# First x rows as four loads, per-channel constants turned by PE, epsilon added by POOL

## The chip, the cores and the metric

The kernel runs on one core of one Trainium2 chip. The time is device microseconds of one execution; the median of three runs of the kernel before is 579.78 us (579.25 to 581.91).

## The reference

Four batches of 512 rows of 512 numbers (x) go through one layer: a gated state-space mixer, whose hidden input is a second tensor (ctx) and whose gate is the normalised x, and then a feed-forward network with weights cut to -1, 0, 1. Both are added to x.

```
h   = in_proj_w @ ctx                                  # 256 -> 512 channels
u   = silu(conv4(h, conv_w) + conv_b)                  # 4 taps per channel, causal
dt, Bm, Cm = split(x_proj_w @ u)                       # 16 + 16 + 16 rows
delta = softplus(dt_proj_w @ dt + dt_proj_b)
state = state * exp(delta * -exp(A_log)) + (delta * u) * Bm      # scan over 512 rows, 16 states
y   = sum_n(state_n * Cm_n) + D * u
x   = x + y * silu(layernorm(x))                       # eps 1e-5
n   = layernorm(x)
g   = silu(quant(n) @ ternary(w_gate)) * (quant(n) @ ternary(w_up))
x   = x + quant(rms_norm(g, ln_w)) @ ternary(w_down)
```

quant rounds each row to 8 bits by its largest absolute value; ternary divides a weight by its mean absolute value, rounds and cuts to [-1, 1].

## The kernel before, in words

Channels lie on the partitions, 4 blocks (KE) of 128; a batch has 512 rows, in 4 blocks (KL) of 128. All engines' programs are written out by hand, one function per engine, and each engine runs its instructions in the order in which they are written; semaphores alone tie them together. SP issues most loads, in one queue.

The opening, some 90 us, prepares everything that the scan wants:

- SP loads the weights of the input projection (in_s), ctx of batch 0, the taps (cw, 512 x 4), the bias (cb, one number per channel), x of batch 0 (load_x(0), one load of 1 MB), and then in turn weights w_all of the feed-forward part (1 MB each), ctx and x of batches 1 to 3 (lines 289 to 310).
- POOL makes the identity and small constants, and then issues eight loads of its own (L416): the projection xp_t in two pieces into xp_s, the delta weights and their bias twice into dt_s, the decay a_log, and D (dsk, one number per channel). xp_s and dt_s were filled with zeros by DVE before (L816, L817; semaphore started). For each batch b it raises the variance plus epsilon to -0.5 (x_power, L432) and normalises x in place (x_norm, L439, 4 instructions). Then it makes skip, the identity scaled by D (L462), and du, the product of delta and u (L449).
- PE projects (conv(b, h), L1096: two channel blocks each, 4 matmuls of 128x512, which run as 8 passes), two calls for each batch, with three pairs of PSUM banks in turn; a pair is free again when DVE has read it. Then come the projection of u (project, L1106), turns and the projection of delta. keep_warm(n) (L1151) are matmuls of ones whose result nobody reads.
- ACT writes the last tap times the projection plus the bias (last_tap, L565), and DVE adds the other three taps (conv, L834: 6 instructions for one call, 12 for a batch). ACT also sums and scales weights (L581, L588), and applies silu (L572). ACT's first wait is for taps and bias (conv_loaded), ahead of everything.
- DVE takes the statistics of x of batch b (x_stats(b): bn_stats L866 four times, bn_aggr L869 four times, epsilon added at L871), and the order on DVE is x_stats(0), both calls of conv of batch 0, x_stats(1), conv of batch 1, x_stats(2), the mean of the first weight, conv(2, 0), x_stats(3), the rest of conv. Behind that it sums and cuts weights (L841, L858, L861), whose stores SP issues, and copies the turned du (L877).

Then the scan runs over 4 batches times 16 states, and the feed-forward part over 16 blocks of rows. Neither is touched by the change, except that the sources of D and of the decay are ready at another time.

## Time and profile before

| what | us |
|---|---|
| median of three runs (lowest, highest) | 579.78 (579.25, 581.91) |
| the profiled execution, its own time | 580.82 |
| its span | 578.9 |
| PE, DVE, ACT, POOL busy | 540.0, 535.8, 512.3, 468.7 |
| mean granted TensorE clock | 0.997 |

The profile is of one execution. The span runs from the first instruction to the last; the execution's own time has the start and the end around it, 1.9 us more. A wait is shown with the engine and line that ended it. The chain of waits follows the work that ended last back to the start. PE's float32 matmuls run as several passes, and each is shown as an instruction; PEld is PE's weight load. The issue of a load (SPq) is short, and its landing is told separately, in us from the issue.

### The profile page before, as it was taken

The page shows a single profiled execution, that of the slowest core. Times are in us where ns is not written, and L with a number is a line of the kernel's source. Part 1 is how long each engine was busy: PE and PEld are TensorE (multiplying, and loading weights), DVE is VectorE, ACT ScalarE, POOL GpSimd, SP SyncE. Part 2 cuts the span into 40 slices and gives each one's busy share as a digit, 9 for nine tenths or more (in the row PEclk, how much of TensorE's full clock was granted, in tenths as well). Part 3 has the DMA queues.
Part 4 walks back from the last instruction along what each step waited for, and adds up shares of the span by engine and source line. Part 5 has one row for each costly group of instructions (what it writes and reads, how often), then busy time and mean ns, then how long its engine had stood idle before and what let it go on. Part 6 is the DMA issues. An engine that isn't in the chain of part 4 may idle for free.

```text
span 578.9 us, 10285 instructions
## 1 busy us (share of the span) xinstructions
PE 540.0 (93%) x3684; PEld 402.5 (70%) x3684; DVE 535.8 (93%) x774; ACT 512.3 (89%) x755; POOL 468.7 (81%) x198
## 2 busy tenths in 40 slices
PE   5898988899999999999999889999989999999996
PEld 2335476899998999989999789987434444444443
DVE  3999989999999999999999999999899989899873
ACT  1899999999999999989999799999877878878784
POOL 4889374999999899999999999995666665765772
PEclk9999999999999999999999999999999999999999
DMA  8992690111222823127432276252442442533521
GB/s 274 410 382 74 217 315 23 55 57 58 66 61 58 196 84 102 55 56 165 128 92 57 63 173 209 74 152 86 78 102 68 96 96 65 109 83 76 116 54 55
DMA packets 62194, 68.64 MB, mean 119 GB/s; under 512 B 41137, under 2 KB 41137, under 8 KB 59969
## 3 DMA queue, kind: packets, MB, share of 16 engines
q1 hardware_dynamic: 59776, 63.59, 36.8%
q0 software_dynamic: 2368, 4.40, 4.6%
q8 instruction: 30, 0.49, 0.3%
q14 instruction: 20, 0.16, 0.1%
HBM read 50.02 MB, written 8.52 MB: 101 GB/s over the span
## 4 chain that ended last, share of the span: by engine, by line
PE 36%; DVE 22%; ACT 20%; POOL 8%; issue 8%; DMA 5%; SPq 0%; DVEq 0%; ACTq 0%; POOLq 0%
PE ps L1268 9%; ACT arena L704 8%; PE ps L1233 8%; POOL arena L473 7%; PE ps L1217 6%; PE ps L1278 6%; ACT arena L629 6%; DVE arena L834 5%; DVE arena L923 5%; PE ps L1220 4%; DMA arena<-c_rows 2%; DVE bst_x L866 2%; DMA arena<-x 1%; ACT arena L626 1%; ACT arena L779 1%
## 5 line engine op out<-in xcount | busy, mean ns | idle before, releaser
L473 POOL TENSOR_TENSOR arena<-arena 128x2048 f32<-128x2048 f32 x62 | 282.2, 4616 | 12.9 <-DVE arena L923 10.1
L923 DVE TENSOR_TENSOR_SCAN arena<-arena,ps 128x512 f32<-128x512 f32 x256 | 286.9, 1197 | 1.8 <-ACT arena L704 0.2
L704 ACT ACTIVATE arena<-arena,a_neg 128x512 f32<-128x512 f32 x256 | 164.9, 709 | 8.2 <-DVE arena L923 8.1
L1233 PE MATMUL ps<-ident,arena 128*128 128x128 f32 x1024 | 155.1, 275 | 6.2 <-DVE arena L933 3.3
L1233 PEld LDWEIGHTS ps<-ident,arena 128*128 128x128 f32 x1024 | 119.9, 141 | 10.4 <-POOL arena L473 5.1
L1268 PE MATMUL ps<-arena 128*128 128x512 bf16 x512 | 113.5, 379 | 1.4 <-DVE arena L1000 0.9
L524 POOL TENSOR_TENSOR arena<-arena 128x1024 f32<-128x1024 f32 x30 | 70.9, 2364 | 49.9 <-DVE arena L1000 49.9
L1217 PE MATMUL ps<-arena 128*128 128x128 f32 x768 | 103.5, 278 | 4.0 <-DVE arena L923 3.8
L629 ACT ACTIVATE arena<-arena,bT 128x512 f32<-128x512 f32 x160 | 101.9, 708 | 1.4 <-PE ps L1220 1.4
L1220 PE MATMUL ps<-ident,arena 128*128 128x128 f32 x640 | 96.2, 274 | 4.2 <-ACT arena L629 2.1
L1217 PEld LDWEIGHTS ps<-arena 128*128 128x128 f32 x768 | 94.4, 194 | 6.2 <-ACT arena L629 2.7
L1268 PEld LDWEIGHTS ps<-arena 128*128 128x128 bf16 x512 | 49.9, 98 | 62.1 <-DVE arena L1000 1.9
L1220 PEld LDWEIGHTS ps<-ident,arena 128*128 128x128 f32 x640 | 73.8, 141 | 7.8 <-issue 4.8
L1278 PE MATMUL ps<-arena 128*128 128x512 bf16 x256 | 58.0, 379 | 3.5 <-DMA arena<-arena 1.5
L779 ACT ACTIVATE arena<-arena,magic,aq 128x2048 f32<-128x2048 f32 x15 | 31.4, 2096 | 27.7 <-DVE aq L964 27.7
L1278 PEld LDWEIGHTS ps<-arena 128*128 128x128 bf16 x256 | 24.1, 98 | 35.6 <-DMA arena<-arena 6.4
L1000 DVE TENSOR_TENSOR arena<-arena,ps 128x512 f32<-128x512 f32 x64 | 43.6, 681 | 1.9 <-PE ps L1268 1.5
L749 ACT ACTIVATE arena<-ps,scales 128x512 f32<-128x512 f32 x64 | 42.0, 677 | 3.7 <-PE ps L1268 3.6
L1096 PE MATMUL ps<-arena 128*128 128x512 f32 x64 | 31.1, 636 | 9.1 <-DMA arena<-ctx_t 8.3
L987 DVE TENSOR_REDUCE half_max<-arena 128x1 f32<-128x1024 f32 x30 | 36.5, 1217 | 2.7 <-POOL arena L524 0.5
L439 POOL TENSOR_SCALAR arena<-arena,mv_x,rstd_x 128x512 f32<-128x512 f32 x16 | 33.0, 2076 | 0.4
L834 DVE SCALAR_TENSOR_TENSOR arena<-ps,cw,arena 128x511 f32<-128x511 f32 (+2 forms) x48 | 31.8, 740 | 0.0
(119 smaller groups left out, 579.8 us busy)
## 6 DMA issues: line engine op xcount, KB each, us to landing
arena<-w_all SPq DMA_DIRECT2D x16, 1024.0 KB, 9.2
arena<-c_rows SPq DMA_DIRECT2D x64, 256.0 KB, 3.3
arena<-x SPq DMA_DIRECT2D x4, 1024.0 KB, 16.2
w_ternary<-arena SPq DMA_DIRECT2D x8, 512.0 KB, 4.3
arena<-w_ternary SPq DMA_DIRECT2D x8, 512.0 KB, 5.0
arena<-x POOLq DMA_DIRECT2D x4, 1024.0 KB, 10.1
out<-arena SPq DMA_DIRECT2D x16, 256.0 KB, 2.0
arena<-ctx_t SPq DMA_DIRECT2D x4, 512.0 KB, 14.1
```

What stands on the lines that cost most here:

```text
L473: nc.gpsimd.tensor_tensor(hs[:, k % RING, :, :], hs[:, k % RING, :, :], c_bc[:, s:s + 1, :].to_broadcast([P, KE, L]), ALU.mult).then_inc(S ...
L524: nc.gpsimd.tensor_tensor(p2[:, s, w], h2[:, s, w], lnw[:, w], ALU.mult).then_inc(S["p2_ready"], 1)
L629: nc.scalar.activation(dB[:, slot(k), i, :], turned[:, b, i, :], ACT.Copy, scale=bT[:, b, i, n:n + 1]).then_inc(S["dB_ready"], 1)
L704: nc.scalar.activation(dA[:, s, i, :], delta_u[:, b, 0, i, :], ACT.Exp, scale=a_neg[:, i, n:n + 1]).then_inc(S["dA_ready"], 1)
L834: nc.vector.scalar_tensor_tensor(out=v[:, k, i:], in0=two("conv", b, h)[:, j, 0:L - i], scalar=cw[:, k, TAPS - 1 - i:TAPS - i], in1=v[:, k ...
L923: nc.vector.tensor_tensor_scan(out=hs[:, k % RING, i, :], data0=dA[:, k % 2, i, :], data1=ps[:, 4 + i, :], initial=0.0, op0=ALU.mult, op1= ...
L1000: nc.vector.tensor_tensor(h2[:, t % 2, j * 512:(j + 1) * 512], sg[:, j % 2, :], ps[:, U_BANK[(t * 4 + j) % 3], :], ALU.mult).then_inc(S["h ...
L1217: last = mm(to, turned[:, k // DS, c, i * P:(i + 1) * P], dgB[:, slot(k), c, :], start=True, stop=True)
L1220: last = nc.tensor.transpose(to, dB[:, slot(k), c, i * P:(i + 1) * P], ident[:])
L1233: last = mm(ps[:, c, i * P:(i + 1) * P], hs[:, k % RING, i, c * P:(c + 1) * P], ident[:], start=(n == 0 and i == 0), stop=(n == DS - 1), i ...
L1268: last = mm(ps[:, bank, :], q1T[:, t, c, :], w[:, c, j * 512:(j + 1) * 512], start=(c == 0), stop=(c == KE - 1))
L1278: last = mm(ps[:, DOWN_BANK[t % 2], :], q2T[:, t % 2, c, :], wd(c), start=(c == 0), stop=(c == KI - 1))
```

## The change

- Batch 0 of x comes as four loads of 256 KB, each with its own semaphore (x0_loaded), and DVE takes the statistics of a block when that block is there. They stand in SP's queue directly behind ctx of batch 0; the loads of the taps and of the bias that stood there are gone.
- Taps, bias and D come as rows: ACT issues three loads into chan_rows, 4 partitions of 512 + 128 + 128 numbers. PE turns them with six transposes into bank 7, and ACT copies them to chan (128 x 24). All who read cw, cb or dsk read chan by tap_of. The consumers wait for chan_ready.
- PE runs seven keep-warm matmuls ahead of the transposes and three behind them. DVE fills the ones for it first.
- POOL loads xp_t in one piece into xp_raw and copies it into xp_s; these loads, and those of the delta weights, now stand behind x_power(0), and the load of the decay behind x_power(2). The load of D is gone.
- Epsilon is added by POOL in x_power, no longer by DVE in x_stats.

```diff
+        xp_raw = part(117, 1)[:, 0:KE * (DR + 2 * DS)].rearrange("p (k n) -> p k n", k=KE)
-        cw = sb("cw", [P, KE, TAPS])
-        cb = sb("cb", [P, KE])
-        dsk = sb("dsk", [P, KE])
+        chan_rows = part(160, 3)[0:KE, :]
+        chan = sb("chan", [P, (TAPS + 2) * KE])
+        def tap_of(i, k):
+            return chan[:, i * KE + k:i * KE + k + 1]
...
             load(in_s, in_t.rearrange("(k p) n -> p k n", p=P), "in_loaded")
             load_ctx(0)
-            load(cw[:], conv_w.rearrange("(k p) n -> p k n", p=P), "conv_loaded")
-            with nc.allow_non_contiguous_dma("one column for each channel"):
-                load(cb[:], conv_b.rearrange("(k p) -> p k", p=P), "conv_loaded")
-            load_x(0)
+            for k in range(KE):
+                sp.dma_start(x_all[:, k, :], x_v[:, 0, k, :]).then_inc(x0_loaded[k], 16)
...
-            xp_v = xp_t.rearrange("(k p) n -> p k n", p=P)
-            pool.wait_ge(S["started"], 2)
-            load(xp_s[:, :, 0:DR], xp_v[:, :, 0:DR], "proj_loaded")
-            load(xp_s[:, :, B_AT:XD], xp_v[:, :, DR:DR + 2 * DS], "proj_loaded")
-            for j in range(2):
-                at = j * XD
-                load(dt_s[at:at + DR, j, :], dt_t, "proj_loaded")
-                load(dt_s[at + DR:at + DR + 1, j, :], dt_b.rearrange("(a n) -> a n", a=1), "proj_loaded")
-            load(a_neg[:], a_log.rearrange("(k p) n -> p k n", p=P), "consts_loaded")
-            with nc.allow_non_contiguous_dma("one column for each channel"):
-                load(dsk[:], d_skip.rearrange("(k p) -> p k", p=P), "consts_loaded")
             def x_power(b):
                 pool.wait_ge(S["x_var"], b + 1)
+                own.done(nc.gpsimd.tensor_scalar(var_x[:, b, :], mv_x[:, b, :, 1], LN_EPS, None, ALU.add))
+                own.wait()
                 nc.gpsimd.tensor_tensor(rstd_x[:, b, :], var_x[:, b, :], mhalf[:, 0:KE],
...
             x_power(0)
+            load(xp_raw, xp_t.rearrange("(k p) n -> p k n", p=P), "xp_loaded")
+            pool.wait_ge(S["started"], 2)
+            for j in range(2):
+                at = j * XD
+                load(dt_s[at:at + DR, j, :], dt_t, "proj_loaded")
+                load(dt_s[at + DR:at + DR + 1, j, :], dt_b.rearrange("(a n) -> a n", a=1), "proj_loaded")
             x_norm(0)
+            pool.wait_ge(S["xp_loaded"], 16)
+            nc.gpsimd.tensor_copy(xp_s[:, :, 0:DR], xp_raw[:, :, 0:DR]).then_inc(S["proj_ready"], 1)
+            nc.gpsimd.tensor_copy(xp_s[:, :, B_AT:XD], xp_raw[:, :, DR:]).then_inc(S["proj_ready"], 1)
             x_power(1)
             x_norm(1)
             x_power(2)
+            load(a_neg[:], a_log.rearrange("(k p) n -> p k n", p=P), "a_loaded")
             x_norm(2)
...
-            act.wait_ge(S["conv_loaded"], 16 * 2)
+            for at, src in ((0, conv_w.rearrange("(k p) n -> k (p n)", p=P)),
+                            (TAPS * P, conv_b.rearrange("(k p) -> k p", p=P)),
+                            ((TAPS + 1) * P, d_skip.rearrange("(k p) -> k p", p=P))):
+                act.dma_start(chan_rows[:, at:at + src.shape[1]], src).then_inc(S["chan_loaded"], 16)
             act.preload_act_table_set("silu_and_others")
+            act.wait_ge(S["chan_psum"], 1)
+            nc.scalar.activation(chan[:], ps[:, 7, 0:(TAPS + 2) * KE], ACT.Copy).then_inc(S["chan_ready"], 1)
+            act.wait_ge(S["chan_ready"], 1)
             last_tap(0, 0)
...
+            step(nc.vector.memset(ones[:], 1.0))
+            nc.vector.memset(magic[:], MAGIC).then_inc(S["dve_consts"], 1)
             nc.vector.memset(xp_s, 0.0).then_inc(S["started"], 1)
             nc.vector.memset(dt_s, 0.0).then_inc(S["started"], 1)
-            step(nc.vector.memset(ones[:], 1.0))
-            nc.vector.memset(magic[:], MAGIC).then_inc(S["dve_consts"], 1)
...
             def x_stats(b):
-                dve.wait_ge(x_loaded[b], 16)
+                if b > 0:
+                    dve.wait_ge(x_loaded[b], 16)
                 for k in range(KE):
+                    if b == 0:
+                        dve.wait_ge(x0_loaded[k], 16)
                     own.done(nc.vector.bn_stats(bst_x[:, k, :], x_all[:, b * KE + k, :]))
...
-                nc.vector.tensor_scalar(var_x[:, b, :], mv_x[:, b, :, 1], LN_EPS, None,
-                                        ALU.add).then_inc(S["x_var"], 1)
+                dve.sem_inc(S["x_var"], 1)
...
             x_stats(0)
+            dve.wait_ge(S["chan_ready"], 1)
             conv(0, 0)
...
+            pe.wait_ge(S["dve_consts"], 1)
+            keep_warm(7)
+            pe.wait_ge(S["consts_set"], 1)
+            pe.wait_ge(S["chan_loaded"], 16 * 3)
+            for i in range(TAPS + 2):
+                rows = chan_rows[:, i:TAPS * P:TAPS] if i < TAPS else chan_rows[:, i * P:(i + 1) * P]
+                last = nc.tensor.transpose(ps[:, 7, i * KE:(i + 1) * KE], rows, ident[0:KE, 0:KE])
+            last.then_inc(S["chan_psum"], 1)
+            keep_warm(3)
             pe.wait_ge(S["in_loaded"], 16)
             conv(0, 0)
...
-            pe.wait_ge(S["proj_loaded"], 16 * 6)
+            pe.wait_ge(S["proj_ready"], 2)
             project(0)
...
+            pe.wait_ge(S["proj_loaded"], 16 * 4)
             delta_in(0, 0)
```

How the built programs stand on three engines. SP's first rows before, and then after the change (arena<-in_t and arena<-ctx_t are the projection's weights and ctx, arena<-w_all the feed-forward weights):

```order
L263 DMA arena<-in_t 128x2x512
L272 DMA arena<-ctx_t 128x2x512
L263 DMA cw<-conv_w 128x4x4
L263 DMA cb<-conv_b 128x4x1
L269 DMA arena<-x 128x4x512
L275 DMA arena<-w_all 128x2048
L272 DMA arena<-ctx_t 128x2x512
L275 DMA arena<-w_all 128x2048
```

```order
L267 DMA arena<-in_t 128x2x512
L276 DMA arena<-ctx_t 128x2x512
L297 DMA arena<-x 128x512 x4
L279 DMA arena<-w_all 128x2048
L276 DMA arena<-ctx_t 128x2x512
L279 DMA arena<-w_all 128x2048
L273 DMA arena<-x 128x4x512
```

The two small loads are gone, and x of batch 0 stands two places earlier, as four.

PE's first rows before and after (ps<-arena 128x512 is the first projection, ps<-ones keep_warm, ps<-ident,arena 128x4 the turn of the rows):

```order
L1096 MATMUL ps<-arena 128x512 [waits ctx_loaded0,in_loaded]
L1096 MATMUL ps<-arena 128x512 x3
L1096 MATMUL ps<-arena 128x512 [waits ctx_loaded0]
L1096 MATMUL ps<-arena 128x512 x3
L1096 MATMUL ps<-arena 128x512 [waits ctx_loaded1]
```

```order
L1161 MATMUL ps<-ones 128x128 [waits dve_consts]
L1161 MATMUL ps<-ones 128x128 x6
L1169 MATMUL ps<-ident,arena 128x4 [waits chan_loaded,consts_set]
L1169 MATMUL ps<-ident,arena 128x4 x5
L1161 MATMUL ps<-ones 128x128 x3
L1106 MATMUL ps<-arena 128x512 [waits ctx_loaded0,in_loaded]
L1106 MATMUL ps<-arena 128x512 x3
```

Sixteen matmuls now stand ahead of the first projection, six of them behind a wait for ACT's loads.

POOL's rows from its first load on, before and after:

```order
L416 DMA arena<-xp_t 128x4x16 [waits started]
L416 DMA arena<-xp_t 128x4x32
L416 DMA arena<-dt_t 16x512
L416 DMA arena<-dt_b 1x16x32
L416 DMA arena<-dt_t 16x512
L416 DMA arena<-dt_b 1x16x32
L416 DMA a_neg<-a_log 128x4x16
L416 DMA dsk<-d_skip 128x4x1
L432 TENSOR_TENSOR rstd_x<-var_x,mhalf 128x4 [waits x_var]
L439 TENSOR_SCALAR arena<-arena,mv_x,rstd_x 128x512 [waits x_rstd]
L439 TENSOR_SCALAR arena<-arena,mv_x,rstd_x 128x512 x3
```

```order
L422 TENSOR_SCALAR var_x<-mv_x 128x4 [waits x_var]
L424 TENSOR_TENSOR rstd_x<-var_x,mhalf 128x4 [waits pool_steps]
L405 DMA arena<-xp_t 128x4x48 [waits x_rstd]
L405 DMA arena<-dt_t 16x512 [waits started]
L405 DMA arena<-dt_b 1x16x32
L405 DMA arena<-dt_t 16x512
L405 DMA arena<-dt_b 1x16x32
L431 TENSOR_SCALAR arena<-arena,mv_x,rstd_x 128x512 x4
L453 COPY arena<-arena 128x4x16 [waits xp_loaded]
L454 COPY arena<-arena 128x4x32
L422 TENSOR_SCALAR var_x<-mv_x 128x4 [waits x_var]
L424 TENSOR_TENSOR rstd_x<-var_x,mhalf 128x4 [waits pool_steps]
```

The first power comes ahead of the loads, five of which stand between it and the first normalisation.

## Rows read from the trace of the kernel before

**Rows 1.** Chain of waits, 0 to 105 us: start us, us, engine, tile, line.

```profile
2.81 8.12 DMA arena<-x
...
10.95 2.48 DVE bst_x L866 x4
...
14.04 7.87 DVE arena L834 x12
...
21.91 2.39 DVE bst_x L866 x4
...
24.91 7.87 DVE arena L834 x12
...
32.77 2.39 DVE bst_x L866 x4
...
42.98 0.23 DVE var_x L871
...
43.20 11.75 DVE arena L834 x18
```

**Rows 2.** Timeline of ACT: start us, us, line, operation, tiles [idle before, releaser].

```profile
27.03 1.91 ACT L581 ACTIVATE arena<-arena 128x2048 bf16<-128x2048 f32 x1 [0.96 <-DMA arena<-w_all]
...
68.65 1.02 ACT L609 ACTIVATE arena<-ps 128x1024 f32<-128x1024 f32 x1 [0.31 <-PE ps L1121]
...
82.38 1.03 ACT L576 ACTIVATE arena<-ps 128x1024 f32<-128x1024 f32 x1 [0.86 <-PE ps L1130]
```

**Rows 3.** Windows: busy us of PE, PEld, DVE, ACT, POOL; PEclk, DMA share, GB/s.

```profile
4.00:5.00 1.00, 0.00 (x0) 0.00 (x0) 0.00 (x0) 0.00 (x0) 1.00 (x3) 1.00 1.05 391
5.00:6.00 1.00, 0.00 (x0) 0.00 (x0) 0.00 (x0) 0.00 (x0) 1.00 (x3) 1.00 1.05 166
6.00:7.00 1.00, 0.87 (x1) 0.50 (x2) 0.00 (x0) 0.61 (x1) 1.00 (x2) 1.00 0.74 252
...
24.00:32.00 8.00, 6.72 (x15) 2.88 (x16) 7.93 (x17) 6.92 (x7) 6.91 (x4) 1.00 1.02 403
```

**Rows 4.** DMA issues by tile, batches 1 and 2, bias, output: KB, us to landing.

```profile
cb<-conv_b SPq DMA_DIRECT2D x1, 2.0 KB, 4.1
...
arena<-x SPq DMA_DIRECT2D x1, 1024.0 KB, 15.0
...
arena<-x SPq DMA_DIRECT2D x1, 1024.0 KB, 17.4
...
out<-arena SPq DMA_DIRECT2D x16, 256.0 KB, 2.0
```

**Rows 5.** Timeline of SP's issues: taps, batches 1 and 2.

```profile
1.75 0.46 SPq L263 DMA_DIRECT2D cw<-conv_w  x1
...
5.65 0.84 SPq L269 DMA_DIRECT2D arena<-x  x1
...
14.85 0.54 SPq L269 DMA_DIRECT2D arena<-x  x1
```

**Rows 6.** POOL's DMA queue, 0 to 60 us: packets, MB, share of 16 engines.

```profile
q0 software_dynamic: 256, 0.20, 1.4%
```

**Rows 7.** Timeline of PE, its weight loads (PEld) and ACT at the first projection.

```profile
6.13 9.16 PE L1096 MATMUL ps<-arena 128*128 128x512 f32 x16 [6.13 <-DMA arena<-ctx_t]
...
8.83 0.34 PEld L1096 LDWEIGHTS ps<-arena 128*128 128x128 f32 x1 [0.52 <-issue]
...
11.27 0.19 PEld L1096 LDWEIGHTS ps<-arena 128*128 128x128 f32 x1 [0.24 <-issue]
...
11.90 1.45 ACT L565 ACTIVATE arena<-ps,cb,cw 128x512 f32<-128x512 f32 x2 [4.23 <-PE ps L1096]
```

**Rows 8.** Timeline of PE: one keep-warm group, six matmuls in 12 passes.

```profile
52.95 1.50 PE L1151 MATMUL ps<-ones 128*128 128x128 f32 x12
```

**Rows 9.** Waits (us, times, longest) to 95 us; POOL's smallest TENSOR_SCALAR by line.

```profile
POOL arena L449 <- DVE arena L861: 13.9, 2, 8.3
...
L496 POOL TENSOR_SCALAR bia<-mv,rstd 128x1 f32<-128x1 f32 x13 | 3.5, 268 | 1.3
```

More of the change, by code:

```diff
@@ L175, in mixer_ffn @@
         wq_dram = nc.dram_tensor("w_ternary", [8, P, INNER], BF16).ap()
-        names = """consts_loaded proj_loaded conv_loaded in_loaded started consts_set dve_consts
+        names = """a_loaded proj_loaded proj_ready in_loaded chan_loaded chan_psum chan_ready xp_loaded started consts_set dve_consts
             in_proj_done tap0_done conv_steps u_ready xdbl_psum xdbl_ready
@@ L188, in mixer_ffn @@
         x_loaded = [sem(f"x_loaded{b}") for b in range(NB)]
+        x0_loaded = [sem(f"x0_loaded{k}") for k in range(KE)]
         x1_added = [sem(f"x1_added{b}") for b in range(NB)]
@@ L400, in _, with load @@
             own = Steps(pool, S["pool_steps"])
+            def load(dst, src, s):
+                nc.gpsimd.dma_start(dst, src).then_inc(S[s], 16)
             own.done(nc.gpsimd.memset(ident[:], 0.0))
@@ L413, in _ @@
                                     pattern=[[0, 1]], channel_multiplier=1).then_inc(S["consts_set"], 1)
-            def load(dst, src, s):
-                nc.gpsimd.dma_start(dst, src).then_inc(S[s], 16)
-            xp_v = xp_t.rearrange("(k p) n -> p k n", p=P)
-            pool.wait_ge(S["started"], 2)
-            load(xp_s[:, :, 0:DR], xp_v[:, :, 0:DR], "proj_loaded")
-            load(xp_s[:, :, B_AT:XD], xp_v[:, :, DR:DR + 2 * DS], "proj_loaded")
-            for j in range(2):
-                at = j * XD
-                load(dt_s[at:at + DR, j, :], dt_t, "proj_loaded")
-                load(dt_s[at + DR:at + DR + 1, j, :], dt_b.rearrange("(a n) -> a n", a=1), "proj_loaded")
-            load(a_neg[:], a_log.rearrange("(k p) n -> p k n", p=P), "consts_loaded")
-            with nc.allow_non_contiguous_dma("one column for each channel"):
-                load(dsk[:], d_skip.rearrange("(k p) -> p k", p=P), "consts_loaded")
             def x_power(b):
                 pool.wait_ge(S["x_var"], b + 1)
+                own.done(nc.gpsimd.tensor_scalar(var_x[:, b, :], mv_x[:, b, :, 1], LN_EPS, None, ALU.add))
+                own.wait()
                 nc.gpsimd.tensor_tensor(rstd_x[:, b, :], var_x[:, b, :], mhalf[:, 0:KE],
@@ L459, in _ @@
             x_norm(3)
-            pool.wait_ge(S["consts_loaded"], 16 * 2)
+            pool.wait_ge(S["chan_ready"], 1)
             for k in range(KE):
-                nc.gpsimd.tensor_scalar(skip[:, k, :], ident[:], dsk[:, k:k + 1], None,
+                nc.gpsimd.tensor_scalar(skip[:, k, :], ident[:], tap_of(TAPS + 1, k), None,
                                         ALU.mult).then_inc(S["skip_ready"], 1)
@@ L565, in last_tap @@
                     nc.scalar.activation(delta_u[:, b, 1, k, :], two("conv", b, h)[:, j, :], ACT.Identity,
-                                         bias=cb[:, k:k + 1],
-                                         scale=cw[:, k, TAPS - 1:TAPS]).then_inc(S["tap0_done"], 1)
+                                         bias=tap_of(TAPS, k),
+                                         scale=tap_of(TAPS - 1, k)).then_inc(S["tap0_done"], 1)
             def silu_u(b):
@@ L612, in decay @@
             def decay():
-                act.wait_ge(S["consts_loaded"], 16 * 2)
+                act.wait_ge(S["a_loaded"], 16)
                 own.done(nc.scalar.activation(a_neg[:], a_neg[:], ACT.Exp))
@@ L1159, in _ @@
             conv(2, 1)
-            pe.wait_ge(S["dve_consts"], 1)
+            pe.wait_ge(S["chan_ready"], 1)
             total(0)
             conv(3, 0)
-            pe.wait_ge(S["proj_loaded"], 16 * 6)
+            pe.wait_ge(S["proj_ready"], 2)
             project(0)
```

2 lines of the change are left out of this document (1 added, 1 removed).

## The prediction

> **What bounds the kernel now.** Read first the chain of waits of the first 105 us [rows 1]. It is one engine's: DVE waits 8.12 us for the first batch of x, and from 10.95 on it works without a hole through the statistics and tap additions of four batches, to 43.20 + 11.75 = 54.95. The reader is to see three starts in it: statistics of batch 0 at 10.95, of batch 1 at 21.91, of batch 2 at 32.77. Behind 55 us DVE cuts weights, and at 82.38 the chain passes to ACT. Read next ACT's own timeline [rows 2]: from 27.03, when a weight load released it, to 81.5 it has one hole, of 0.31 us, and then waits 0.86 us at 82.38. So two nearly equal paths lead to 82.38, DVE's and ACT's, and an edit gives the end only what it gives both. What lies behind (scan, FFN) starts when these paths end; no line of it changes in work or order, so I take it to move as a block.
>
> The third reading is of the transfers. In the windows of the opening [rows 3] the DMA engines move 391 GB/s from 4 to 5 us, then 166 and 252. The landings [rows 4], added to their issues [rows 5], say which load is late: batch 1 lands at 5.65 + 15.0 = 20.65 (DVE takes it 1.26 later, at 21.91), batch 2 at 14.85 + 17.4 = 32.25 (taken only 0.52 later, at 32.77). From 24 to 32 us they move 403 GB/s [rows 3]: the queue is full there, so a load lands earlier only if something ahead of it goes.
>
> **The change, part by part.** *Loads.* The taps and the bias, 1,024 pieces of 16 and 4 bytes, stood in SP's queue ahead of batch 0. In the two windows that show them (391 - 166) + (391 - 252) = 364 GB/s are missing for 1 us each: 364/391 = 0.93 us of full-rate moving, my price for removing both; the bound below is nothing (rival C). On POOL's queue (0.20 MB, 1.4% of 16 engines in 60 us, that is 0.84 us [rows 6]) D's load goes, the projection's two loads become one behind the first x_power, the four of the delta weights come behind it, and the decay's load moves behind the third x_power, near 36 us, past batch 2. I take half of the 0.84 out of what stands ahead of batch 2; the bounds are none and all of it. Sum for the loads from batch 1 on: 0.93 + 0.42 = **1.35 us earlier**, between 0.9 and 1.8.
>
> *Batch 0 as four loads.* They are issued from 1.75 us on, where the taps stood [rows 5]. The first two loads (1 MB) are done at 6.13, where PE starts [rows 7]; a quarter of batch 0 (256 KB) then takes 0.67 us at 391 GB/s. They land at about 6.8, 7.5, 8.2 and 8.8, and DVE has the statistics done near 9.9, four microseconds earlier. DVE then waits for taps: what is late next is the first projection.
>
> *The rows turned by PE.* ACT issues three small loads, one per 0.46 us (an issue of SP's [rows 5]), the last at 1.7. No load of ACT's stands in the trace; its bounds are an output store's 2.0 us and the bias' 4.1 [rows 4]: landed at 3.7 to 5.8. I take 4.5, nearer the short one, since little is queued on ACT itself. PE runs 7 keep-warm matmuls (14 passes) from about 1.3; twelve such passes take 1.50 [rows 8], so it takes 1.75, or 3.5 at half speed: to 4.8, which covers the landing. Six transposes at that 0.125 are 0.75 to 1.5, three more keep-warm matmuls the same. The projection starts between 6.3 and 7.8; I take 7.0, 0.9 later than now.
>
> *Its pace.* The weight loads inside the first projection come every 0.86 us (0.34 + 0.52) to past 9 us, and later every 0.43 [rows 7]. The windows call the granted clock 1.00 throughout [rows 3], but by this pace the array ran at the lower level (1.2 GHz) first and at 2.4 GHz then. PE had done nothing before 6.13. Now it will have worked since 1.3, so I take the short pace for all eight passes: 3.44 us in place of 5.77 (6.13 to 11.90, where ACT takes it [rows 7]). It ends at 10.4, ACT's last tap 0.73 later (1.45 for two), and DVE adds taps from **11.2 instead of 14.04**. The Trainium skill (TensorE: Matmul & The Clock Gate, Part 1) has the idle state throttled and calls idleness what throttles again; a wait for the rows between the two keep-warm groups is such idleness. By that the taps would start 2.3 us later, at 13.5. The rows agree on the start from idle; of a short wait within work they show nothing.
>
> *Onward.* Batch 0's taps take 7.87: to 19.1. Batch 1 lands at 20.65 - 1.35 = 19.3. Its statistics take 2.80 (24.91 - 21.91, less 0.20 for the removed epsilon) and its taps 7.87: DVE stands at batch 2 at 30.0. That load lands at 32.25 - 1.35 = 30.9. So of the 2.8 us only 32.77 - 30.95 = 1.8 survive: **the bound is then batch 2's landing**. The two later epsilon additions (0.17, and 0.23 [rows 1]) add 0.4: DVE is 2.2 ahead at 43.20 and after. ACT is 1.35 ahead, since a load releases it at 27.03: its work ends at 81.52 - 1.35 = 80.2. DVE's path reaches 82.38 - 2.2 = 80.2. The 0.86 us at 82.38 close, and both paths give **2.2 us**.
>
> *Costs set at nothing.* POOL adds epsilon four times (0.27 each [rows 9]). Between the first power and the first normalisation it now issues five loads, 2.3 us at SP's price and perhaps more; but the power comes four microseconds earlier, so the normalisation is not later. The two copies behind it must be done when PE projects u, which waits for batch 1's taps (24.91 + 7.87 = 32.8 now), some ten microseconds later. Later POOL waits up to 8.3 us at a time for weight cuts [rows 9]; that is the cover. If it went, POOL's 4 us would stand ahead of PE's turning of du. ACT's issues, table load and copy lie ahead of last taps that PE cannot feed before 10.4. DVE's reordered fills lie within its 8 us of waiting for batch 0.
>
> Sum: span 578.9 - 2.2 = 576.7. The profiled execution took 580.82, 1.04 above the median of three runs, 579.78; from the median the forecast is **577.6 us**. About 0.5% (2.9 us) is what a measurement of this kernel can tell from no change.
>
> **The rivals.**
>
> *A. The rows come late, and it gets slower.* Place: the wait for chan_loaded, with the first projection, all last taps and DVE's taps queued behind it. If ACT's loads share the way with x and end as x does, 8.12 us after issue [rows 1], they land at 9.8; 0.75 for the transposes, 0.75 for warming, 3.44 and 0.73 behind it: taps start at 15.5, and at 17.8 with the long pace. Batch 2's statistics follow 18.54 us behind that (7.87 + 2.80 + 7.87), at 34.0 to 36.3 against 32.77, less 0.4: 0.9 to 3.2 us slower, some 581.8. It decides from taps at 14.6 on, so from rows landed at 8.9, or at 6.6 with the long pace. Against it: the bias, queued behind 1 MB, took only 4.1. The Trainium skill (DMA: Bandwidth & Descriptors, Queues, rings and completion order) lets an engine alternate between the rings of SP and ACT, which speaks against A, and a semaphore's write land only behind every earlier write of its engine, which speaks for it; no row here has a load of ACT's.
>
> *B. Rows as late as the bias (5.8), and the long pace.* 5.8 + 1.5 + 5.77 + 0.73: taps at 13.8, batch 2 at 32.3, less 0.4: 0.8 us gained, 579.0.
>
> *C. The small pieces cost no time.* The dip of rows 3 may be another load starting up. Then batch 2 lands at 32.25 still: DVE gains its 0.52 + 0.4, ACT its 0.86: 578.9.
>
> *D. The transfers gain more.* If POOL's packets cost SP's queue more than their own time, say 1.3 us, the loads land 2.2 earlier, DVE finds batch 2 at its arrival at 30.0 and is 2.8 + 0.4 = 3.2 ahead, ACT 2.2 + 0.86 = 3.1: 576.7. Against: the delta weights' loads still stand ahead of batch 2.
>
> *E. The change doesn't carry.* Its 0.31 and 0.86 us of holes ACT makes itself with PE, so that they stay, and the gain is ACT's 1.35 or less: 578.4 to 579.
>
> **How the numbers follow.** Forecast 0.42, D 0.22, E 0.12, C 0.11, B 0.08, A 0.05. The forecast's own range is 577.1 to 578.0 (1.8 and 0.9 on the loads give 2.7 and 1.8). With D below, C, E and B above, and half a microsecond at either end for the median's scatter, it is 576.1 to 579.4. Faster by over 0.5% lies below 576.9: two thirds of D, and 0.12 of the forecast by that scatter, 0.27 together. Slower by over 0.5% (582.7) is the long pace of A and what I don't see, 0.04. The rest, 0.69, is no difference that can be told.
>
> **What would show it.** Right: first tap addition near 11.2; DVE idle before batch 2's statistics, ended by the load of x at 30.9; taps done near 52.7; ACT released by the weight load near 25.7; no window under 350 GB/s between 4 and 8 us; everything behind 82 us earlier by 2.2. Wrong in the first step: PE idle over 1 us behind its first keep-warm group, or projection passes at 0.86. Wrong in the second: batch 2 landed at 32 still. Wrong in the last: the first 82 us shorter by 2 us and the span not.

## The result, and the profile after

| kernel | median us (lowest to highest) | ratio to before, 95% interval |
|---|---|---|
| before, in the same comparison | 580.17 (578.76 to 583.22) | |
| the change | 585.46 (581.4 to 589.13) | 1.0077 [1.0055, 1.0098] |

The forecast was 577.6 us, at most 579.4. The change is 5.3 us slower by the medians, 4.5 by the ratio. Its profiled execution took 586.47 us with a span of 584.7, against 578.9.

First the opening. Chain of waits of the changed kernel, answering to [rows 1]:

```profile
1.62 4.06 DMA arena<-d_skip
...
8.22 14.95 PE ps L1106 x32
23.25 1.46 ACT arena L565 x2
24.76 7.96 DVE arena L841 x12
32.73 2.39 DVE bst_x L876 x4
...
43.08 0.09 issue
43.16 11.90 DVE arena L841 x18
...
73.65 5.88 DMA w_ternary<-arena
...
80.93 1.06 PE ps L1150 x8
81.99 3.11 PE ps L1140 x16
```

The reader is to see that 24.76, 32.73 and 43.16 are the old starts 24.91, 32.77 and 43.20: nothing was won by 55 us. The chain now leads through the first projection, where it had led through x. Behind it stand a store of 5.88 us and PE's turning in 3.11. The timelines of PE, of its weight loads and of DVE say why, answering to [rows 7]:

```profile
1.17 3.35 PE L1161 MATMUL ps<-ones 128*128 128x128 f32 x14 [1.17 <-DVE magic L824]
5.81 0.83 PE L1169 MATMUL ps<-ident,arena 4*128 4x4 f32 x6 [1.29 <-DMA arena<-d_skip]
6.57 1.65 PE L1161 MATMUL ps<-ones 128*128 128x128 f32 x6
8.01 5.28 PE L1106 MATMUL ps<-arena 128*128 128x512 f32 x9
...
9.72 0.34 PEld L1106 LDWEIGHTS ps<-arena 128*128 128x128 f32 x1 [0.52 <-issue]
...
10.98 0.19 PEld L1106 LDWEIGHTS ps<-arena 128*128 128x128 f32 x1 [0.24 <-issue]
...
13.86 7.97 DVE L841 SCALAR_TENSOR_TENSOR arena<-ps,chan,arena 128x511 f32<-128x511 f32 x12 [3.20 <-ACT arena L565]
21.74 2.46 DVE L876 BATCH_NORM_STATS2 bst_x<-arena 128x6 f32<-128x512 f32 x4
```

PE waits 1.29 us for the rows, which land at 5.68, and its passes keep the long pace (0.86 us each) to past 10 us, as in the kernel before. DVE's taps start at 13.86; by the same view they started at 13.95 (the chain of [rows 1] gives that start as 14.04).

The windows of the opening in the changed kernel (columns as in [rows 3]) and its landings show that the transfers did come earlier:

```profile
5.00:6.00 1.00, 0.19 (x2) 0.22 (x2) 0.00 (x0) 0.00 (x0) 0.00 (x0) 1.00 0.84 249
6.00:7.00 1.00, 1.00 (x8) 0.98 (x8) 0.00 (x0) 0.19 (x1) 0.00 (x0) 1.00 0.99 371
...
80.00:88.00 8.00, 7.07 (x50) 7.11 (x51) 5.72 (x5) 4.52 (x6) 4.96 (x3) 0.79 0.77 276
```

```profile
arena<-x SPq DMA_DIRECT2D x1, 1024.0 KB, 14.1
...
arena<-x SPq DMA_DIRECT2D x1, 1024.0 KB, 18.7
```

The landings answer to [rows 4]. Issued at 5.28 and 12.42, batches 1 and 2 land at 19.4 and 31.1 (20.65 and 32.25 before). DVE is not there to take them. The window from 5 to 6 us still stands at 249 GB/s, though, where the prediction wanted none under 350. ACT's last wait ahead of the scan, 0.86 us in [rows 2], is longer too:

```profile
85.12 1.02 ACT L576 ACTIVATE arena<-ps 128x1024 f32<-128x1024 f32 x1 [3.48 <-PE ps L1140]
```

Then the part that "moves as a block". The first scan instruction of DVE starts at 95.82 (93.35 before, 2.47 later), the scan ends 3.41 later, the span 5.8 later. So 2.5 us are lost from 55 to 96 us, 0.9 in the scan, 2.4 in the feed-forward part. None of these three places has changed code. The waits of PE from 400 to 590 us (us, times, longest), of the kernel before and then of the changed one:

```profile
PE ps L1278 <- DMA arena<-arena: 1.5, 1, 1.5
```

```profile
PE ps L1298 <- DMA arena<-arena: 4.3, 3, 1.6
```

These are waits for the turns that the DMA engines make of q2, the rounded input of the last product: of the 30 DMA_TRANSPOSE in a trace these are 14, some 10 us apart, and they alone are meant by "turn" below. (The other 16 turn q1, the rounded input of the first products.) A turn takes 4.3 us to landing; in the changed kernel two took longer. DMA issues in windows that hold one turn each: 449 to 450 us before, then 452 to 454 and 537 to 538.5 of the change.

```profile
arena<-arena SPq DMA_TRANSPOSE x1, 4.3
```

```profile
arena<-arena SPq DMA_TRANSPOSE x1, 5.8
...
arena<-arena SPq DMA_TRANSPOSE x1, 6.0
```

What lies in the long ones is a transfer of another queue. Queues of the changed kernel from 455 to 458 us, and of the kernel before from 456 to 458:

```profile
q1 hardware_dynamic: 1451, 0.36, 141.4%
q8 instruction: 1, 0.02, 1.9%
```

```profile
q8 instruction: 1, 0.02, 2.9%
```

Queue q8 brings program: 30 packets in the whole run, 0.49 MB, so 16 KB each. It keeps one DMA engine busy for 0.93 us. PE has 3,693 + 3,710 instructions in the page, so there is one packet for each 250 or so. In the kernel before the packet came when the turn that started at 449.20 had long landed; in the changed one it came at 456.2, 3.3 us into the turn of 452.88.

It holds up more than the one DMA engine that brings it. Windows of the changed kernel from that moment on, and of the kernel before at the same distance (3.6 to 4.1 us) behind the start of its turn of 449.20 (the last number is GB/s):

```profile
456.50:457.00 0.50, 0.50 (x4) 0.24 (x3) 0.22 (x2) 0.50 (x3) 0.50 (x1) 1.00 4.88 74
457.00:457.50 0.50, 0.47 (x3) 0.00 (x0) 0.35 (x2) 0.50 (x2) 0.50 (x2) 1.00 0.06 6
457.50:458.00 0.50, 0.00 (x0) 0.00 (x0) 0.50 (x1) 0.37 (x1) 0.50 (x1) 1.00 0.14 23
458.00:458.50 0.50, 0.00 (x0) 0.00 (x0) 0.50 (x2) 0.00 (x0) 0.39 (x2) 1.00 1.35 270
```

```profile
452.80:453.30 0.50, 0.50 (x4) 0.27 (x3) 0.21 (x2) 0.50 (x3) 0.50 (x1) 1.00 1.13 211
```

For a microsecond the core's 16 DMA engines together move next to nothing, and all 16 shares of the turn land late (from 5.63 us on). Why one engine's packet stops the others' is not shown.

Working hypothesis: the 26 passes (52 instructions) that the change adds ahead of the first projection shift these loads against everything else.

### The profile page after: what moved, and what is told of

The parts are those of the page before. It is cut to its first block, busy times and chain, and to the rows that moved or that the text cites. A ratio compares the mean times of both kernels' runs of the same rounds, so it can differ in the third digit from the quotient of the medians.

```text
span 584.7 us, 10332 instructions
## 1 busy us (share of the span) xinstructions
PE 545.3 (93%) x3693; PEld 410.8 (70%) x3710; DVE 536.8 (92%) x770; ACT 513.2 (88%) x756; POOL 470.9 (81%) x202
## 4 chain that ended last, share of the span: by engine, by line
PE 31%; ACT 22%; DVE 21%; issue 9%; POOL 9%; DMA 7%; ACTq 0%; DVEq 0%; POOLq 0%
ACT arena L711 8%; POOL arena L475 8%; PE ps L1253 7%; PE ps L1237 6%; ACT arena L629 5%; PE ps L1288 5%; DVE arena L933 5%; PE ps L1298 4%; DVE arena L841 4%; PE ps L1240 4%; DMA arena<-c_rows 3%; PE ps L1106 3%; ACT arena L786 2%; DMA arena<-arena 2%; ACT arena L756 2%
## 5 line engine op out<-in xcount | busy, mean ns | idle before, releaser
L841 DVE SCALAR_TENSOR_TENSOR arena<-ps,chan,arena 128x511 f32<-128x511 f32 (+2 forms) x48 | 31.9, 739 | 3.5 <-ACT arena L565 3.2
L1106 PE MATMUL ps<-arena 128*128 128x512 f32 x64 | 29.9, 619 | 2.1 <-DVE arena L841 1.8
## 6 DMA issues: line engine op xcount, KB each, us to landing
arena<-x POOLq DMA_DIRECT2D x4, 1024.0 KB, 10.5
arena<-ctx_t SPq DMA_DIRECT2D x4, 512.0 KB, 12.9
```

What stands on the lines that cost most here:

```text
L841: nc.vector.scalar_tensor_tensor(out=v[:, k, i:], in0=two("conv", b, h)[:, j, 0:L - i], scalar=tap_of(TAPS - 1 - i, k), in1=v[:, k, i:], o ...
```

## The experiments

Ratios are to the kernel before, run beside each; its median lay between 580.2 and 581.5. "Hits" are turns of the feed-forward part that hold a 16 KB load and take 5.7 us or more in the profiled execution. "First scan" is the start of DVE's first scan instruction against 93.35, in the profiled execution too. The kernel before has no hit.

| kernel | us | ratio, interval | first scan | hits |
|---|---|---|---|---|
| the change | 585.46 | 1.0077 [1.0055, 1.0098] | +2.47 | 2 |
| the change again, one execution | 585.29 | | +1.27 | 2 |
| before + 26 passes | 583.04 | 1.0041 [1.0024, 1.0059] | +0.19 | 1 |
| change, no early keep-warm | 582.27 | 1.0027 [1.0005, 1.0048] | +0.38 | 1 |
| change, 10 keep-warm in one piece | 583.21 | 1.0047 [1.0029, 1.0066] | -1.78 | 2 |
| change, 26 passes fewer later | 582.18 | 1.0021 [1.0005, 1.0037] | +0.22 | 1 |
| 10 in one piece, and 26 fewer later | 580.82 | 0.9999 [0.9986, 1.0011] | -0.72 | 1 |
| before, 26 passes fewer | 583.38 | 1.0036 [1.002, 1.0053] | +0.56 | 2 |
| 10 in one piece, groups 1, 1, 0 | 582.03 | 1.0003 [0.9986, 1.0019] | -1.15 | 2 |
| the same, groups 0, 0, 0 | 580.40 | 0.9984 [0.9968, 1.0] | -1.10 | 2 |
| the same, groups 2, 1, 1 | 579.77 | 0.9976 [0.9962, 0.999] | -1.46 | 0 |
| the same, groups 1, 1, 1 | 580.87 | 0.9998 [0.9981, 1.0014] | -1.64 | 2 |
| before + 8 passes at 421 us | 583.46 | 1.0035 [1.0017, 1.0054] | -0.25 | 1 |

**The place alone, by more passes.** The kernel before with 13 small matmuls whose result nobody reads, at a place where PE has time:

```diff
             conv(1, 1)
+            pe.wait_ge(S["dve_consts"], 1)
+            for _ in range(13):
+                mm(ps[:, 6, 0:4], ones[:], ones[:, 0:4], start=True, stop=True)
             conv(2, 0)
             conv(2, 1)
-            pe.wait_ge(S["dve_consts"], 1)
```

> The kernel before, with 26 PE passes of no use (13 matmuls of ones, 4 columns) in the hole of about 1.9 us ahead of conv(2, 0); nothing else differs. Theory P: the change is slower because its 26 more PE instructions move the loads of PE's program (16 KB each on one DMA engine, 81.2 us before, 76.5 after) into the store that DVE and PE wait for at 74 to 78 us. Then this kernel is slower too: 584 to 585 us, a program load near 76.5, the last of the store's 16 shares landing over 1 us behind the 15th, and a stretch at half clock near 82 us. Theory R: the loss comes from the edits themselves (ACT's loads, POOL's epsilon, four loads of x); then this kernel stays at 580 us, within 0.2%.

Measured 1.0041 [1.0024, 1.0059], 583.04 us. The opening is as before (+0.19 us at the first scan), yet the kernel is slower by half of what the change costs. Some loads moved much as in the change (from 49.3 to 41.5 us, from 98.9 to 91.0; the change has 40.8 and 94.4), but the one that I had expected near 76.5 stayed at 81.6 (81.2 before): the store takes 4.62, no half clock follows, and 584 to 585 us was missed. What is slower here comes later. One turn, from 449.38, holds the load of 453.5 and takes 6.01 us.

**Without the early keep-warm.**

```diff
-            keep_warm(7)
...
-            keep_warm(3)
```

> The changed kernel without its ten keep-warm matmuls (7 and 3) in the opening: PE has 6 instructions more than before, in place of 26. Theory P: the program load returns to near 80 us, behind the store, and the time to 579 to 580.5 us. The first projection starts where its load lands, near 6.7 instead of 8.0, at the long pace as before, and DVE's taps near 12.9. Theory R: it stays at 585 us.

Measured 1.0027 [1.0005, 1.0048]. The projection starts at 6.65, 1.4 us earlier than in the change, but in the long pace until 12.7; the taps start at 14.31 (I had expected 12.9), and the first scan is 0.38 later than before. It is 3 us faster than the change: the store at 74 us takes 4.38 again, there is no half clock near 82 us, and one hit in place of two. So the early keep-warm as written bought 0.45 us at the taps (13.86 against 14.31), and nothing against the kernel before (13.95), while its instructions cost more than that. The 579 to 580.5 us that I expected were missed: one hit is left.

**The hole in the warm-up closed.** All ten matmuls ahead of the transposes, so that PE works until the rows are there:

```diff
-            keep_warm(7)
+            keep_warm(10)
...
-            keep_warm(3)
```

> The changed kernel with its ten keep-warm matmuls in one group ahead of the rows' turn, so that PE works from 1.2 us to the projection with almost no hole (the changed kernel had one of 1.29 us at 4.5); the number of PE instructions is that of the change. If the hole kept PE at the long pace, the projection now runs at 0.43 us per pass from its start near 7 us, it ends near 10.5, and DVE's taps start near 11.5 instead of 13.9. If the hole has nothing to do with it, the projection goes on at 0.86 to about 10.5 us and DVE's taps start near 13.3. Theory P: the program load stays near 76.5 us, and the time near 584 us. Theory R: it gains what the opening gains, up to 1 us, from 585.

PE's timeline of this kernel and its weight loads:

```profile
1.17 4.63 PE L1161 MATMUL ps<-ones 128*128 128x128 f32 x20 [1.17 <-DVE magic L824]
5.74 0.83 PE L1169 MATMUL ps<-ident,arena 4*128 4x4 f32 x6
6.59 5.82 PE L1106 MATMUL ps<-arena 128*128 128x512 f32 x13
...
7.09 0.19 PEld L1106 LDWEIGHTS ps<-arena 128*128 128x128 f32 x1 [0.24 <-issue]
```

DVE's of the same kernel:

```profile
11.26 7.96 DVE L841 SCALAR_TENSOR_TENSOR arena<-ps,chan,arena 128x511 f32<-128x511 f32 x12 [0.87 <-ACT arena L565]
19.16 2.47 DVE L876 BATCH_NORM_STATS2 bst_x<-arena 128x6 f32<-128x512 f32 x4
...
30.88 2.47 DVE L876 BATCH_NORM_STATS2 bst_x<-arena 128x6 f32<-128x512 f32 x4 [0.73 <-DMA arena<-x]
```

This is the opening that the prediction drew: passes of 0.43 us from the start, taps at 11.26, and a wait for x that ends at 30.88 (forecast 11.2 and 30.9). The first scan comes 1.78 us earlier than before. And still the kernel takes 1.0047: with the same instructions ahead it has two hits as the change has, and in the profiled execution its scan is 1.8 us longer than that of the kernel before (POOL waits 4.8 us for c_rows in it, 2.9 before). The store is free of a load this time (79.5 us, behind its landing).

**Fewer passes later, so that the place is as before.** The three keep-warm groups ahead of delta_in lose 13 matmuls, 26 passes: in the change, in the kernel with ten in one piece, and in the kernel before.

```diff
-            keep_warm(6)
+            keep_warm(2)
...
-            keep_warm(6)
+            keep_warm(2)
...
-            keep_warm(6)
+            keep_warm(1)
```

> The changed kernel with 13 keep-warm matmuls (26 passes) taken out of the three groups of six at 45 to 54 us, so that PE's program is as long as before from the scan on. Theory P2: the 16 KB loads of PE's program, each some 0.95 us on one DMA engine, cost 1.2 to 1.7 us where one falls into the 4.3 us of a transposing store that PE waits for (456.2 and 541.5 us in the changed kernel, 453.5 with 26 passes added to before, none of that size in before); their place follows the count of PE's instructions. Then the loads in the feed-forward part stand as before (7 to 8 us behind the start of a transposing store), no such store takes over 5 us, and the time is 580 to 581.5 us in place of 585.5. Theory R2: the edits themselves cost it, or the clock does; then it stays above 584 us.

Measured 1.0021 [1.0005, 1.0037] against the change's 1.0077: 3.3 us come back with the work of the opening untouched. The load that fell on the store is at 81.4 us, the store takes 4.73, no half clock near 82. One hit is left, which I had not expected, and with it 580 to 581.5 us were missed.

> As the run before, on the version with its ten keep-warm matmuls in one group (its first scan began 1.8 us earlier than before). Theory P2: the 1.8 us of the opening reach the end: 578.5 to 579.5 us, faster than before by 0.2 to 0.35%. Theory R2: no better than that version, 583 us.

Measured 0.9999 [0.9986, 1.0011], 2.4 us less than its sister without the thinning, but not the 578.5 to 579.5 us expected. One hit is a part of that; another is that ten matmuls in one piece didn't bring the short pace in this execution. Its weight loads:

```profile
9.45 0.34 PEld L1106 LDWEIGHTS ps<-arena 128*128 128x128 f32 x1 [0.52 <-issue]
10.23 0.19 PEld L1106 LDWEIGHTS ps<-arena 128*128 128x128 f32 x1 [0.44 <-issue]
```

The projection went on at 0.86 us per pass to 10.1, though PE had worked from 1.17 to 6.6 without a hole, and the taps start at 13.10. In the five other traces with ten in one piece the projection has the short pace from its second pass on, and taps at 11.20 to 11.46.

> The kernel before with the same 13 keep-warm matmuls taken out, nothing else: PE's program is 26 passes shorter than before. It separates what the thinned groups do by themselves. Theory P2: the program loads move by the same amount the other way, so some other transfer may be hit: between 579.5 and 584 us, and whatever the time is, each transposing store of over 5 us has a 16 KB load in it. Theory R2: 580 to 581 us, as before. If the thinned groups let PE's clock fall, a stretch at half clock stands at 50 to 60 us and adds 1 to 2 us here and in the two runs above.

Measured 1.0036 [1.002, 1.0053]: slower than before although it does less. Two turns hold a load (5.92 and 5.96 us). Moving PE's program 26 passes either way costs the kernel before 0.4%: its own places, without a hit, are lucky. Nor does leaving the thirteen matmuls out gain anything ahead of the scan, which starts 0.56 us later.

**Small doses.** The kernel with ten in one piece and groups 2, 2, 1, less three, five, one and two keep-warm matmuls. The third of them:

```diff
             keep_warm(2)
...
-            keep_warm(2)
+            keep_warm(1)
...
             keep_warm(1)
```

> e5_warm10_thin with three more keep-warm matmuls left out ahead of delta_in (groups of 2, 2, 1 become 1, 1, 0), which are 12 instructions of PE (a load and a pass each, two passes a matmul). Theory of the place (PE's 16 KB program loads come every so many instructions, and one that falls within the some 4.3 us of a turn by transposing DMA costs PE 1.2 to 1.7 us): in e5 a load was at 483.5 us, 3.9 us behind a turn's start, in the kernel before at 488.6, behind a turn's end. Leaving 12 instructions out moves the loads a little later, to some 486 to 487; it sits within or just behind the turn's end, so one hit fewer or the same: 579.0 to 580.8. Rival (the work in the opening alone counts, the place of the loads does not): 580.8, and the same long turns at the same moments.

> As e7, with all three keep-warm groups ahead of delta_in left out (5 matmuls fewer than e5, 20 instructions). Theory of the place: loads of the feed-forward part at some 488 and 541 us as in the kernel before, no turn over 5.0 us that holds a 16 KB load, PE waits on turns below 2 us in 400 to 590, 578.5 to 579.8, if no load of the opening falls on a store that is waited for, and if PE keeps its clock without these groups. Rival (idle time in place of keep-warm lowers the clock): a stretch at half clock before 90 us and 582 or more. Rival (place does not count): 580.8.

> e5_warm10_thin (groups 2, 2, 1) with one keep-warm matmul fewer (2, 1, 1), 4 instructions of PE. In e5 the 16 KB loads of the feed-forward part stood at 426.9, 483.5 and 509.5 us, the second 3.9 behind a turn's start; in e7 (12 instructions fewer) at 431.2, 488.6 and 516.1, the first and the last 3.6 and 3.7 behind one. Theory of the place: this one's stand between, and whichever of them begins 3 to 4.2 us behind a turn's start makes that turn 5.7 us or longer and costs PE 1.2 to 1.7 us; with one such turn 580.3, with none 578.8, with two 581.5. Rival (the trace's long turns and the loads coincide by chance): a turn over 5.5 us with no 16 KB load in it, or a load 3 to 4.2 us behind a start with a turn of 4.3.

> As e10, with two keep-warm matmuls fewer than e5 (1, 1, 1), 8 instructions. Theory of the place: loads between those of e5 and e7; none, one or two of them 3 to 4.2 us behind a turn's start give 578.8, 580.3 or 581.5, and each such turn is 5.7 us or longer. Rival (coincidence): as for e10. Rival (only the opening counts): 580.6 for both of these kernels, as e5, e7 and e8 were within 0.2% of the kernel before.

In the first two the loads moved as foreseen, 483.5 to 488.6 and 487.3, out of that turn. I had not foreseen that two others (431.2 and 516.1; 430.6 and 515.4) would then fall 3.6 to 3.9 us into a turn, so both missed the times I gave for them (582.03 and 580.40 measured). One matmul fewer is the dose without a hit (loads at 427.6, 455.9, 487.3, 510.0 and 539.0): 579.77 us, 0.9976 [0.9962, 0.999], the only kernel of the study whose interval lies below one (I had given 578.8 for no hit). With two hits the last kernel gives that back: 580.87 us (581.5 given). The ratios between these four differ by little more than their intervals, so that they follow the hits is not shown by the times; the traces show what a hit does (below). And hits don't explain all: the kernel with ten in one piece and the last one have the same opening (-1.78 and -1.64 us at the first scan) and two hits each, yet 1.0047 and 0.9998. In their traces the scan makes the difference, 304.5 and 301.5 us.

**The change once more.**

> The changed kernel once more, one look. Theory of the place: the loads fall at the same instructions, so the same three events repeat: a 16 KB load near 76.5 us within the store that ends at 79.5, and two turns of the feed-forward part over 5.7 us, at some 453 and 538. Rival (chance of one execution): the store near 73.7 takes 4.7 us, or the long turns stand elsewhere. The stretch at half clock near 82 us should repeat if PE's idle time of 3.1 us ahead of it is its cause.

The loads came at 76.4, 455.2 and 539.4 us, the store took 5.79, the turns 5.94 and 6.26: they came again in the second execution of the same program, so they aren't the chance of one. The half clock near 82 us did not repeat, although PE's wait ahead of it did. PE's timeline in the change, and then in this execution:

```profile
80.93 1.06 PE L1150 MATMUL ps<-ident,arena 128*128 128x128 f32 x8 [3.10 <-DVE arena L886]
81.83 3.26 PE L1140 MATMUL ps<-ident,arena 128*128 128x128 f32 x16
```

```profile
80.82 1.06 PE L1150 MATMUL ps<-ident,arena 128*128 128x128 f32 x8 [2.99 <-DVE arena L886]
81.72 1.91 PE L1140 MATMUL ps<-ident,arena 128*128 128x128 f32 x16
```

So of the 2.47 us at the first scan 1.2 are the store, in both, and 1.2 the half clock, in one.

The opening, too, went another way to the same end. Here the clock rose at 4.1 us, and after PE's wait of 1.76 us for the rows the three keep-warm matmuls ran at the short pace; then it fell to one half from 7.5 to 10.9, under the projection. A window of this execution (the third last number is the granted clock):

```profile
8.00:11.00 3.00, 3.00 (x5) 1.04 (x4) 2.60 (x8) 0.00 (x0) 0.22 (x1) 0.52 1.05 425
```

The change with 26 passes fewer later, whose opening is the same, did so as well (half clock from 7.9 to 11.3 behind a hole of 1.60). In the first execution of the change the clock had not risen at all before the hole: its fourteen keep-warm passes came every 0.21 us, at the long pace. The taps start at 13.85 to 13.86 in all three.

**Eight passes in the feed-forward part.** The cleanest test: the kernel before, with nothing changed up to 421 us.

```diff
                     if j == 2 and tile(t - 2) and t < END:
+                        if t == 2:
+                            for _ in range(4):
+                                mm(ps[:, DOWN_BANK[0], 0:4], ones[:], ones[:, 0:4], start=True, stop=True)
                         turned_by_dma(t - 2)
```

> The kernel before with four matmuls of ones (4 columns, 8 passes, 16 instructions of PE with their loads) at one place of the feed-forward part: ahead of PE's wait for the first turn, where it is idle 1.53 us in the trace of the kernel before. Opening and scan are untouched, to 421 us. Nothing else can move but the place of PE's later 16 KB program loads, which in the kernel before all begin 7 to 8 us behind a turn's start or just ahead of one. Theory of the place: they come some 4 us earlier, and at least one then falls 3.3 to 4.1 us behind a turn's start; that turn takes 5.7 to 6.3 us in place of 4.33, PE waits 1.2 to 1.7 us for it, and the kernel is 1.5 us slower for one such turn, 3 for two (ratio 1.0025 to 1.005). Rival (the place costs nothing, the long turns come from elsewhere): 8 passes hidden in 1.53 us of idle time, ratio 1.000, turns of 4.3.

The scan starts 0.25 us earlier and ends within 0.02 us of the kernel before, and these turns start within 0.13 us of its own up to the one at 480.86. The 16 KB load comes at 484.9 in place of 488.6. DMA issues in the window 480 to 482, before and then here:

```profile
arena<-arena SPq DMA_TRANSPOSE x1, 4.4
```

```profile
arena<-arena SPq DMA_TRANSPOSE x1, 6.1
```

PE behind that turn, before and then here:

```profile
485.19 2.98 PE L1278 MATMUL ps<-arena 128*128 128x512 bf16 x13
```

```profile
486.99 1.25 PE L1278 MATMUL ps<-arena 128*128 128x512 bf16 x5 [1.74 <-DMA arena<-arena]
```

Of the 1.74 us that PE waits, 0.8 reach the next turns (0.10 us later than before up to there, 0.94 from the turn at 502.74 on), and the span is 1.05 longer. The measured ratio 1.0035 is 2.0 us, its interval 1.0 to 3.1. So the hit costs about 1 us in the trace, which is the lower end of what the times say; whether the rest is more than scatter is open. That a kernel gets slower by the place of a program load alone is shown.

**All turns together.** The 14 traces hold 196 such turns:

| the turn holds | turns | us to landing |
|---|---|---|
| a 16 KB load (q8), begun 3.3 to 4.1 us behind its start | 19 | 5.75 to 6.26 |
| an 8 KB load (q14), begun 3.6 to 4.1 behind | 8 | 4.82 to 5.13 |
| neither of these, or a load begun within 1.4 us of its start or ahead | 169 | 4.24 to 4.42 |

There is no exception. In three of the 19 an 8 KB load lies in the same turn, the one of 6.26 among them; without these the longest is 6.09. PE waits 0.96 to 1.92 us at each of the 19 and up to 0.7 at those with an 8 KB load alone. (Its wait of 1.5 us at the first turn is in every trace, with no load in it; the eight passes above fill half of it.) The kernel's time follows: from the last scan instruction to the end of the span it takes 182.9 and 183.8 us in the two traces without a hit, 183.3 to 184.5 in the five with one, 184.6 to 187.0 in the seven with two. The 8 KB loads don't move with PE's instructions: with 26 more passes one is at 117.0 us in place of 116.8, where the 16 KB ones before and behind it moved by 2 and 4 (112.3 to 110.2, 127.9 to 123.7). I take them for other engines' program. The store near 73 us is the same story: 4.38 to 4.84 in the twelve traces in which the 16 KB load begins from 79.5 us on, 5.88 and 5.79 in the two in which it begins at 76.5 and 76.4. In the change 15 of its 16 shares had landed by 78.3, one at 79.53: a store waits for the one share behind the load, where in 17 of the 19 long turns all 16 shares came late.

## Why the prediction was wrong

- *"Sum for the loads from batch 1 on: 1.35 us earlier"*: right in size, 19.4 and 31.1 against 19.3 and 30.9. The account of it is shown in part only: 249 and 371 GB/s stand where 166 and 252 stood, which is 0.52 us at 391 GB/s and not 0.93, so the rest came from elsewhere. The blocks of batch 0 landed at 7.5 to 9.5 and not at 6.8 to 8.8; nothing waited for that.
- *The rows turned by PE, "I take 4.5, nearer the short one"*: the first step that failed. The rows landed at 5.68, 4.06 from the last issue, where the bias had taken 4.1. The nearest row was that of another small load in the opening, not of an output store; rival B had it.
- *"Now it will have worked since 1.3, so I take the short pace for all eight passes"*: failed with it. Seven keep-warm matmuls ended at 4.5 and left a hole of 1.29 us; the long pace went on to 10.5, much as before. Closing the hole (ten in one piece) gave 0.43 us passes from the second on and taps at 11.26, and so in five of six traces; in the three traces with the hole the long pace stands from its second pass on. The sentence beside it, by the Trainium skill (TensorE: Matmul & The Clock Gate, Part 1), named this very idleness and 13.5 us for the taps; they came at 13.86. The second execution agrees with it (up at 4.1 us, a hole, one half from 7.5 on); in the first the clock had not yet risen when the hole came. The rule deserved a rival with a chance of its own. B, with late rows and the long pace, gave 13.8.
- *"the bound is then batch 2's landing"*: not reached in the change (DVE came at 32.64 to 32.73, when x had landed at 31.1); right as soon as the hole was closed (30.88).
- *"The two later epsilon additions add 0.4"*: wrong. From the statistics to the taps of batch 1 it takes 21.74 to 24.76, 3.02 us, against 3.00. DVE's own wait and its semaphore instruction took the addition's place.
- *"I take it to move as a block"*: the step that turned no gain into a loss: at 55 us the change stood where the kernel before had stood, and all 5.8 us of its profiled execution came behind that. Even with the opening as drawn, 1.78 us ahead at the first scan, the kernel was slower (1.0047), and with the change's own opening and 26 passes fewer behind it 3.3 us came back. No rival had it: I counted what PE's 26 passes cost in time, and not that they are 52 instructions, which move 16 KB program loads onto a store and two turns that PE waits for: 1.2 us and about 1.2 each in the trace, in place of the nothing that I had put there.
- The account of the profiled execution's 5.8 us: 1.2 for the store, 1.2 for the half clock that followed in this one, 0.9 in the scan, 2.4 behind it for two hits (PE waits 2.8 us longer for turns). The second execution has no such half clock and 4.6 us.

What stays open: the scan, 0.9 us of the change's loss and as much as 3 us between two kernels of equal opening and hits. Its length over the traces goes with POOL's waits for c_rows (301.5 to 304.5 us with 2.2 to 4.8 us of waits; 302.7 with 2.9 before, 303.6 with 4.2 in the change), but these transfers also share the engines with weights and x, and I could not tie each wait to a load. Nor was it tried to say what of the remaining difference between kernels with equally many hits (the one with groups 0, 0, 0 and the one with 1, 1, 0) is the clock, whose half-speed stretches came at other times in nearly every execution. How the number of instructions gives the moment of a load was not worked out either; places were found by trial.

## What to carry to other kernels

When a kernel waits for transfers all along, count the instructions that an edit adds to the busiest program, not only their time: look where the "instruction" queue's packets fall against the transfers that somebody waits for, and compare a change with a padded twin of the kernel before, or part of what is read as its merit is the luck of its place. Warm-up work is worth its place only if it lasts until the real work starts: ten matmuls in one piece did, in five traces of six, what seven and three around a wait did in none of three. For a load of a queue that has none in the trace, take the landing of a small load of the same stage.

## What the runs showed of the hardware

- One 16 KB program packet takes one DMA engine 0.93 us (the one of the changed kernel at 456.2), and lengthens a turn that it falls into by 1.4 to 1.9 us (4.33 to 5.75 and up to 6.26), more than its own time, since meanwhile all 16 engines move next to nothing (6 and 23 GB/s in the two halves of the microsecond from 457.0, 211 in the turn without it); an 8 KB one lengthens it by 0.5 to 0.8. In a store only the one share behind the packet is late.
- All 27 loads that lengthened a turn began 3.3 to 4.1 us behind its start; none of the others began between 1.4 and 3.3, so what a load does there is not shown by these turns (packets of the turn, and of the turn of q1 issued behind it, move from 1.2 to 4.4 us behind its start). The second turn of q1, near 384 us, fills the gap: it took 4.48 to 5.40 us in the nine traces with a 16 KB load begun 2.0 to 3.4 us in, and 3.37 to 3.65 in the five others.
- The clock column says 1.00 for the windows from 4 to 8 us in both kernels, while the passes at 0.86 and 0.43 us show the two levels (1.2 and 2.4 GHz). In both traces the first record of the clock begins only where the pace turns short, at 10.3 us before and 10.5 in the change (6.4 with ten in one piece); ahead of it the column has no record and says 1.00. At the start the pace of the weight loads is the witness.
- Six 4-partition transposes take 0.83 us, and the last of ACT's three small loads at the start (2 KB) lands 4.06 and 4.37 us behind its issue in the two executions of the change.
